# Later steps of x in 256-byte runs, a ring of three half units, one output tile, small ScalarE loads behind its copies

## The chip, the cores and the metric

One Trainium2 chip, one core. The metric is device time in microseconds (us) of one execution of the program, as the median of several runs. All data is float32; "f32r" tiles hold float32 values that TensorE reads in its one-pass float32 form.

## The reference, cut to what matters

x is [B=128, T=64, D=512]; `cond` is [128, 512] and serves twice: as the 128 taps of a depthwise causal convolution and as the initial state of a GRU.

```python
x = x + (depthwise_causal_conv(x, taps=cond[:, None, :]) + conv_b)   # 128 taps over 64 time steps
gi = x_t @ W_ih + b_ih ; gh = h @ W_hh + b_hh                         # for t in 0..63, one after the other
r = sigmoid(i_r + h_r); z = sigmoid(i_z + h_z); n = tanh(i_n + r * h_n)
h = (1 - z) * n + z * h
out[:, t] = x_t + h
```

Here x_t is the x after the convolution. The 64 GRU steps depend on each other through h; the convolution depends on nothing but the input.

## The kernel before, in words

**GRU steps.** Each of the 64 steps multiplies the state and the next step's x with two 512 x 1536 matrices. Every float32 product is done as three TensorE matmuls on a high and a low part (hi*hi, hi*lo, lo*hi; `block_product`, L775 to L781). A step is 24 groups of three matmuls of 512 columns, 72 in all, on L779, and four transposes of h (L741). ScalarE makes the high part of h and of the next x (L605, L571), the sigmoids and the tanh (L578, L591, L586), and puts the biases into the PSUM banks (L519). VectorE makes the low parts (L617), the gate arithmetic (L697 to L708), the residual sum `outT` (L723) and its transposition `outZ` (L730). SP stores outZ in four DMAs (`store_out`, L402) and loads the x of the step four ahead in four more (`load_early_xT` L328, `load_xT` L336). There are two `outZ` tiles used in turn; a transposition waits for the store of two steps earlier.

**Time steps 0 to 15 of the convolution (the early part)** are computed before the first step, 64 channel groups on TensorE (L768, 16 banks of 4 groups), from a Toeplitz tile that ScalarE and VectorE build out of the taps (L500, L641). The taps go through DRAM first: `tap_pad` is stored and `tap_blocks` loaded by ScalarE's DMA queue (L467 to L472), which then also issues four loads of `bias_d` (L476) and two of `bias_pair` (L481), before ScalarE's first copy (L485). The results are stored to `early` in DRAM in four quarters (L325) and come back transposed as xT(t) (L330).

**Time steps 16 to 63 (the bulk)** are computed between the matmuls of GRU steps t = 1 to 13. Channels go in pairs (two channels are stacked on the 128 partitions, 64 time steps each), two pairs to a PSUM bank: 128 banks m = 0 to 127, ten to a step, at the points p = 0 to 9, which come after 3, 5, 8, 10, 12, 15, 17, 20, 22 and 24 of the 24 groups (the transposes of h stand after the 20th). m = 10 (t - 1) + p. `bulk` (L786) issues four matmuls for a bank (L801). A **block** j is four pairs, that is banks 2j and 2j + 1. For each block

- SP loads the Toeplitz matrices from DRAM in two DMAs of 128 KB, runs of 256 bytes (`load_toep`, L352, L358), into a ring of four; the load for block m/2 + 3 is issued at bank m;
- ScalarE rounds x to its high part (L551) and VectorE subtracts to get the low part (L668), `split(j)`, into a ring of three; at bank m = 2j - 4, whose point in the step is even;
- each bank is emptied by ScalarE (L561, two halves into `tmp`, adding the bias) and VectorE (L679, into `stage`); TensorE may use bank m when bank m - 3 has been emptied.

x comes in **units**: 32 pairs, that is 2 x 32 channels, in 8 DMAs of 256 KB (`load_x_quarter`, L343, L347), so runs of 32 channels = 128 bytes, into two tiles `x_unit` used in turn. Units 0 and 1 are loaded before the loop; quarters of a later unit go out one at a time at every second bank, from the bank at which the unit two back has been split. `stage` holds eight banks, twice; `store_stage` (L364) writes it to `xres` in DRAM in two DMAs at banks m with m % 8 == 2, the stage of the eight banks before, and VectorE waits for the store of two stages back before it writes the first bank of a new one (L677).

**Order on SP.** SP's program is one list: at each point of step t the bulk loads and stores above (each behind its wait on `conv_done`, which counts finished banks), then `store_out(t)` behind the wait for outZ, then the x of step t + 4. Before the loop: xT(1), unit 0 of x (8 DMAs), four toeps (8), xT(2) and xT(3) (8), unit 1 of x (8).

**Order on ScalarE at the points** (VectorE's is the same with `second_half`): p0: split, first_half; r and its bias; first_half(p1); split(p2), first_half(p2); wait for the pre-activation, tanh, bias of i_n; first_half(p3); wait for the z product, z, two biases; split(p4), first_half(p4), first_half(p5); split(p6), first_half(p6); split(p8), first_half(p7); high part of h; first_half(p8).

Of the kernel before, what the change touches and what calls it, by code (L numbers as in the profile page):

```python
# [5 lines left out]
P = 128  # L6
# [3 lines left out]
ACT = mybir.ActivationFunctionType  # L10
# [9 lines left out]
def conv_residual_gru(  # L20
# [26 lines left out]
    KB = D // P  # L47
# [12 lines left out]
    UNIT = 32  # L60
    NUNIT = PAIRS // UNIT
    STAGE = 16
# [37 lines left out]
    x_unit = [place(f"x_unit{n}", B * UNIT) for n in range(2)]  # L100
# [10 lines left out]
    xT2, xT3 = place("xT2", D), place("xT3", D)  # L111
    gru_end = top[0]
    xT0, xT1 = place("xT0", D), place("xT1", D)
# [14 lines left out]
    top[0] = toep_at  # L128
# [4 lines left out]
    assert top[0] <= gru_end  # L133
# [18 lines left out]
    with ctx:  # L152
# [48 lines left out]
        x_unit_loaded = [sem(f"x_unit_loaded{n}") for n in range(2)]  # L201
# [29 lines left out]
        out_stored = [sem(f"out_stored{n}") for n in range(2)]  # L231
# [53 lines left out]
        def x_block(j):  # L285
            c0 = j % (UNIT // BLOCK) * BLOCK
            unit = j // (UNIT // BLOCK) % 2
            return x_unit[unit][:, :].rearrange("p (b g) -> p g b", g=UNIT)[:, c0:c0 + BLOCK, :]

        def part_block(j, low):  # L290
            return parts[j % HL_RING][:, :].rearrange("p (g l b) -> p g l b", l=2, b=B)[:, :, low, :]
# [4 lines left out]
        def _(sp):  # L296
# [81 lines left out]
            for b4 in range(4):  # L378
                load_x_quarter(0, b4)
# [4 lines left out]
            for b4 in range(4):  # L384
                load_x_quarter(1, b4)

            def bulk(t, point):
# [491 lines left out]
```

## Time and profile before

| what | us |
|---|---|
| median of 3 runs | 1238.42 (1237.55 to 1242.0) |
| the profiled execution: its time | 1239.42 |
| the profiled execution: its span | 1237.5 |
| TensorE matmul busy in the span | 1182.9 (96%) |
| TensorE weight load busy | 986.4 (80%) |
| VectorE / ScalarE busy | 539.3 / 500.2 |
| data moved | 97.98 MB in 288354 packets, 212752 of them under 512 bytes |

Time outside the span is 1.9 us. Engines in the rows below: PE is TensorE's matmuls, PEld its weight loads, DVE VectorE, ACT ScalarE, POOL GpSimd, SPq and ACTq the DMA issues of SyncE and ScalarE. L779 is line 779 of the kernel. A PSUM bank appears as "bank". Each window row gives the stretch, its length, then busy us (and instructions) of PE, PEld, DVE, ACT and POOL, the mean granted TensorE clock (1.00 is 2.4 GHz), the busy share of the 16 DMA engines and GB/s.

### The profile page before, as it was taken

The numbers are of one execution on the slowest core, as the hardware profiler recorded it, in microseconds if no ns is written. First come the engines' busy times: TensorE is split into PE (matmuls) and PEld (weight loads), VectorE is DVE, ScalarE is ACT, GpSimd is POOL, SyncE is SP. The second block draws the span as 40 slices with busy tenths as digits, with TensorE's granted clock in tenths as the row PEclk, the third lists the DMA queues.
The fourth block names the chain that finished last, engine by engine and source line by source line (L and its number), as shares of the span: only waits on it lengthen the run. The fifth ranks groups of instructions, "written<-read, shape, count | busy, mean of one in ns | idle before, by whom it ended". The sixth has DMA issues, their size and how long they took to land.

```text
span 1237.5 us, 15341 instructions
## 1 busy us (share of the span) xinstructions
PE 1182.9 (96%) x5518; PEld 986.4 (80%) x5518; DVE 539.3 (44%) x811; ACT 500.2 (40%) x934; POOL 17.2 (1%) x19
## 2 busy tenths in 40 slices
PE   1997999899989999999999999999999999999997
PEld 1976788787878888888888888888888888888886
DVE  2835766476655333333333333333333333333333
ACT  4436766576755333323333323333332333332332
POOL 0400000000000000000000000000000000000000
PEclk9999999899989999999999999999999999999999
DMA  9978888788853111111011111001111101111100
GB/s 244 293 176 161 167 173 175 170 183 174 173 149 77 54 32 35 34 34 32 24 29 34 34 34 34 25 25 34 34 34 34 28 24 34 34 34 34 32 17 21
DMA packets 288354, 97.98 MB, mean 79 GB/s; under 512 B 212752, under 2 KB 282384, under 8 KB 286272
## 3 DMA queue, kind: packets, MB, share of 16 engines
q1 hardware_dynamic: 283968, 96.29, 33.1%
q10 hardware_dynamic: 4352, 1.25, 0.4%
q8 instruction: 20, 0.33, 0.1%
q14 instruction: 14, 0.11, 0.0%
HBM read 63.34 MB, written 34.14 MB: 79 GB/s over the span
## 4 chain that ended last, share of the span: by engine, by line
PE 89%; ACT 3%; issue 2%; SPq 2%; DMA 2%; DVE 2%; ACTq 0%; DVEq 0%
PE bank L779 80%; PE bank L801 4%; PE bank L741 2%; PE bank L768 2%; SPq L347 1%; ACT tmp L561 1%; ACT x_parts L551 1%; SPq L358 1%; DMA early<-early_result 1%; ACT bank L519 0%; ACT toep_early L500 0%; DMA xres<-stage 0%; DVE stage L679 0%; DVE x_parts L668 0%; DMA tap_pad<-tap_rows 0%
## 5 line engine op out<-in xcount | busy, mean ns | idle before, releaser
L779 PE MATMUL bank<-w_ih_hi,xT_hi 128*128 128x512 f32 x768 | 308.2, 401 | 0.0
L779 PE MATMUL bank<-w_ih_hi,xT_lo 128*128 128x512 f32 x768 | 302.2, 394 | 0.0
L779 PE MATMUL bank<-w_ih_lo,xT_hi 128*128 128x512 f32 x768 | 302.2, 393 | 0.0
L779 PE MATMUL bank<-w_hh_hi,hT_hi 128*128 128x512 f32 x768 | 299.6, 390 | 0.0
L779 PE MATMUL bank<-w_hh_lo,hT_hi 128*128 128x512 f32 x768 | 299.5, 390 | 0.0
L779 PE MATMUL bank<-w_hh_hi,hT_lo 128*128 128x512 f32 x768 | 298.8, 389 | 0.0
L779 PEld LDWEIGHTS bank<-w_ih_hi,xT_lo 128*128 128x128 f32 x768 | 145.6, 190 | 31.8
L779 PEld LDWEIGHTS bank<-w_hh_hi,hT_lo 128*128 128x128 f32 x768 | 144.2, 188 | 30.4
L779 PEld LDWEIGHTS bank<-w_ih_hi,xT_hi 128*128 128x128 f32 x768 | 146.1, 190 | 27.2 <-ACT bank L519 0.4
L779 PEld LDWEIGHTS bank<-w_ih_lo,xT_hi 128*128 128x128 f32 x768 | 146.1, 190 | 26.8
L779 PEld LDWEIGHTS bank<-w_hh_hi,hT_hi 128*128 128x128 f32 x768 | 144.4, 188 | 28.1
L779 PEld LDWEIGHTS bank<-w_hh_lo,hT_hi 128*128 128x128 f32 x768 | 144.4, 188 | 27.6
L617 DVE TENSOR_TENSOR hT_lo<-bank,hT_hi 128x512 fp32r<-128x512 f32 x64 | 44.1, 688 | 219.7 <-ACT hT_hi L605 219.3
L697 DVE TENSOR_TENSOR q<-bank,r 128x512 f32<-128x512 f32 x64 | 44.2, 690 | 204.6 <-PE bank L779 203.4
L605 ACT ACTIVATE hT_hi<-bank 128x512 fp32r<-128x512 f32 x63 | 37.7, 599 | 206.1 <-PE bank L741 206.1
L586 ACT ACTIVATE n_gate<-q 128x512 f32<-128x512 f32 x64 | 40.5, 633 | 172.6 <-DVE q L699 172.6
L801 PEld LDWEIGHTS bank<-x_parts,toep_ring 128*128 128x128 f32 x512 | 79.4, 194 | 36.7 <-issue 20.1
L801 PE MATMUL bank<-x_parts,toep_ring 128*128 128x256 f32 x512 | 84.6, 289 | 22.0 <-issue 18.2
L561 ACT ACTIVATE tmp<-bank,bias_pair 128x128 f32<-128x128 f32 x256 | 78.3, 364 | 54.8 <-PE bank L801 54.5
L571 ACT ACTIVATE xT_hi<-xT 128x512 fp32r<-128x512 f32 x63 | 39.8, 632 | 123.6 <-PE bank L779 108.3
L668 DVE TENSOR_TENSOR x_parts<-x_unit,x_parts 128x512 fp32r<-128x512 f32 x64 | 70.2, 1097 | 44.7 <-ACT x_parts L551 44.6
L551 ACT ACTIVATE x_parts<-x_unit 128x512 fp32r<-128x512 f32 x64 | 73.8, 1155 | 24.0 <-PE bank L801 21.2
(59 smaller groups left out, 802.3 us busy)
## 6 DMA issues: line engine op xcount, KB each, us to landing
x_unit<-in_x_dram SPq DMA_DIRECT2D x64, 256.0 KB, 4.7
toep_ring<-kernel_parts SPq DMA_DIRECT2D x128, 128.0 KB, 3.3
out_dram<-outZ SPq DMA_DIRECT2D x256, 64.0 KB, 1.6
xres<-stage SPq DMA_DIRECT2D x32, 384.0 KB, 5.0
xT<-xres SPq DMA_DIRECT2D x192, 64.0 KB, 1.9
early<-early_result SPq DMA_DIRECT2D x4, 1024.0 KB, 13.8
xT<-early SPq DMA_DIRECT2D x60, 64.0 KB, 2.0
w_ih_raw<-in_L_cond_W_ih_dram SPq DMA_DIRECT2D x12, 256.0 KB, 7.8
```

Of the source, the lines that this page charges most:

```text
L551: nc.scalar.activation(part_block(j, 0), x_block(j), ACT.Copy).then_inc(x_hi_ready, 1)
L561: nc.scalar.activation(tmp[m % 2][:, pair * B:(pair + 1) * B], conv_bank[m % 3][:, pair * 2 * B:pair * 2 * B + B], ACT.Identity, bias=bias ...
L571: nc.scalar.activation(xT_hi[:, :], xT[(u + 1) % RING][:, :], ACT.Copy).then_inc(xT_hi_ready, 1)
L586: nc.scalar.activation(n_gate[:, :], q[:, :], ACT.Tanh).then_inc(n_ready, 1)
L605: nc.scalar.activation(hT_hi[:, :], ps_hT[:, :], ACT.Copy).then_inc(hT_hi_ready, 1)
L617: nc.vector.tensor_tensor(lo_out[:, :], full[:, :], hi_in[:, :].bitcast(F32), ALU.subtract).then_inc(lo_ready, 1)
L668: nc.vector.tensor_tensor(part_block(j, 1), x_block(j), part_block(j, 0).bitcast(F32), ALU.subtract).then_inc(x_lo_ready, 1)
L697: nc.vector.tensor_tensor(q[:, :], ps_hn[:, :], r[:, :], ALU.mult).then_inc(reset_h_ready, 1)
L741: mm = nc.tensor.transpose(psum[:, k * P:(k + 1) * P], source[:, k * P:(k + 1) * P], ident[:, :])
L768: mm = nc.tensor.matmul(conv_bank[n % 3][:, slot:slot + B], toep_early[:, g * P:(g + 1) * P], x_early[:, :].rearrange("p (b g) -> p g b", ...
L779: mm = nc.tensor.matmul(psum[:, :], a[:, rows], b[w][:, cols], start=False, stop=stop and n == 2, skip_group_check=True)
L801: mm = nc.tensor.matmul(conv_bank[m % 3][:, pair * 2 * B:(pair + 1) * 2 * B], toep[j % T_RING][:, at:at + P], parts[j % HL_RING][:, slot * ...
```

## The change

Four things.

1. **Units of 64 pairs.** UNIT goes from 32 to 64, so a run of x is 256 bytes and there are four units instead of eight. Instead of two unit tiles there is a ring of three tiles of half a unit, split over the batch (64 of the 128 rows each). A half is four DMAs of 512 KB, each with as many runs as one of before. Units use the tiles (0,1), (0,2), (1,2), (0,1). Before the loop go unit 0 (8 DMAs, where unit 0 of before had 8 smaller ones) and the second half of unit 1 (4 DMAs, in place of 8). Later halves go out four DMAs at once: the first half of unit 1 at bank 27, behind a wait for the low part of block 15; the first of unit 2 at bank 30; the second of unit 2 at bank 59, behind block 31; the first of unit 3 at bank 62; the second of unit 3 at bank 91, behind block 47. The first three blocks of units 1 to 3 are split 1, 2 and 3 banks ahead of their first bank instead of 4, so split(16), split(32), split(48) stand at banks 31, 63 and 95, points p1, p3 and p5. `x_block` and `part_block` get one more dimension for the two halves.
2. **STAGE goes from 16 to 8**: `stage` holds four banks, twice; its store is half as large and goes out at m % 4 == 2.
3. **Output tiles.** `outT` is the tile q, which the gates use too, and one `outZ` takes the place of two; VectorE waits for outZ of the step before ahead of q, and the transposition for the store of the step before.
4. **Before the loop.** ScalarE copies x_row (L485) ahead of its first DMA issues, and makes the copies of L489 to L493 ahead of the six small loads of `bias_d` and `bias_pair`. TensorE no longer waits for `y0_ready` before the early matmuls, only before the third bank, which is the PSUM bank that y0 is read from.

Cut to its core:

```diff
-    UNIT = 32
+    UNIT = 64
     NUNIT = PAIRS // UNIT
-    STAGE = 16
+    UNIT_BLOCKS = UNIT // BLOCK
+    HALF = B // 2 * UNIT
+    HALF_OF = ((0, 1), (0, 2), (1, 2), (0, 1))
+    HALF_USE = ((1, 1), (2, 1), (2, 2), (3, 3))
+    STAGE = 8
...
-    x_unit = [place(f"x_unit{n}", B * UNIT) for n in range(2)]
+    x_ring = place("x_ring", 3 * HALF)
...
-    outT = place("outT", D)
     r, z, n_gate, q = (place(n, D) for n in ("r", "z", "n_gate", "q"))
-    outZ = [place(f"outZ{n}", D) for n in range(2)]
+    outT = q
+    outZ = place("outZ", D)
...
         def split_block(t, point):
             m = bulk_bank(t, point)
-            if m is None or m % 2 or m // 2 + 2 >= NBLOCK:
+            if m is None:
                 return None
-            return m // 2 + 2
+            for j in (m // 2 + 2, (m + 3) // 2, (m + 1) // 2):
+                ahead = (1, 2, 3)[j % UNIT_BLOCKS] if j % UNIT_BLOCKS < 3 and j >= UNIT_BLOCKS else 4
+                if 2 * j - ahead == m and j < NBLOCK:
+                    return j
+            return None
...
-            def load_x_quarter(unit, b4):
-                for c in range(2):
-                    ch = unit * 2 * UNIT + c * UNIT
-                    bs = slice(b4 * B // 4, (b4 + 1) * B // 4)
-                    sp.dma_start(
-                        x_unit[unit % 2][c * T:(c + 1) * T, :].rearrange("s (b g) -> s b g", g=UNIT)[:, bs],
-                        x[bs, :, ch:ch + UNIT].rearrange("b s g -> s b g"),
-                    ).then_inc(x_unit_loaded[unit % 2], 16)
+            def load_x_half(unit, half):
+                n = HALF_OF[unit][half]
+                for part in range(2):
+                    b0 = half * B // 2 + part * B // 4
+                    for c in range(2):
+                        ch = unit * 2 * UNIT + c * UNIT
+                        cols = slice(n * HALF + part * HALF // 2, n * HALF + (part + 1) * HALF // 2)
+                        sp.dma_start(
+                            x_ring[c * T:(c + 1) * T, cols].rearrange("s (b g) -> s b g", g=UNIT),
+                            x[b0:b0 + B // 4, :, ch:ch + UNIT].rearrange("b s g -> s b g"),
+                        ).then_inc(x_half_loaded[n], 16)
...
-            for b4 in range(4):
-                load_x_quarter(0, b4)
+            for half in range(2):
+                load_x_half(0, half)
             for j in range(T_RING):
                 load_toep(j)
             load_early_xT(2)
             load_early_xT(3)
-            for b4 in range(4):
-                load_x_quarter(1, b4)
+            load_x_half(1, 1)
...
-                if m % 8 == 2 and m > 2:
-                    store_stage(m // 8 - 1)
-                unit, b4 = (m + 21) // 16, (m + 21) % 16 // 2
-                if m % 2 and 2 <= unit < NUNIT and b4 < 4:
-                    if b4 == 0:
-                        sp.wait_ge(x_lo_ready, (unit - 1) * UNIT // BLOCK)
-                    load_x_quarter(unit, b4)
+                if m % 4 == 2 and m > 2:
+                    store_stage(m // 4 - 1)
+                unit = (m + 5) // 32
+                if 1 <= unit < NUNIT:
+                    if (m + 5) % 32 == 0:
+                        sp.wait_ge(x_lo_ready, unit * UNIT_BLOCKS)
+                        load_x_half(unit, 0 if unit == 1 else 1)
+                    if (m + 5) % 32 == 3 and unit < NUNIT - 1:
+                        load_x_half(unit + 1, 0)
...
-                unit = j // (UNIT // BLOCK)
-                act.wait_ge(x_unit_loaded[unit % 2], 16 * 8 * (unit // 2 + 1))
+                if j % UNIT_BLOCKS == 0:
+                    for half in range(2):
+                        act.wait_ge(x_half_loaded[HALF_OF[j // UNIT_BLOCKS][half]],
+                                    16 * 4 * HALF_USE[j // UNIT_BLOCKS][half])
...
+                if isinstance(i, bass.RuntimeValue) or t > 0:
+                    dve.wait_ge(outZ_ready, t)
                 dve.wait_ge(gh_n_done, t + 1)
...
-                if isinstance(i, bass.RuntimeValue) or t >= 2:
-                    dve.wait_ge(out_stored[u % 2], 16 * QUADS * (2 * i + u // 2))
-                nc.vector.transpose(outZ[u % 2][:, :], outT[:, :]).then_inc(outZ_ready, 1)
+                if isinstance(i, bass.RuntimeValue) or t > 0:
+                    dve.wait_ge(out_stored, 16 * QUADS * t)
+                nc.vector.transpose(outZ[:, :], outT[:, :]).then_inc(outZ_ready, 1)
...
-            pe.wait_ge(y0_ready, KB)
             for g in range(G0):
                 n, slot = g * B // BANK, g * B % BANK
                 if slot == 0 and n >= 3:
                     pe.wait_ge(early_evicted, n - 2)
+                if slot == 0 and conv_bank[n % 3] is ps_x0 and n < 3:
+                    pe.wait_ge(y0_ready, KB)
```

## Rows read from the trace of the kernel before

**Rows 1.** The page's fourth section: the chain that ended last, by engine

```profile
PE 89%; ACT 3%; issue 2%; SPq 2%; DMA 2%; DVE 2%; ACTq 0%; DVEq 0%
```

**Rows 2.** Windows: steps 2 to 12 together, then steps 6, 7, 9 and 11

```profile
117.74:379.22 261.48, 247.24 (x1278) 210.20 (x1276) 165.25 (x265) 176.31 (x375) 0.00 (x0) 0.97 0.79 168
208.80:237.80 29.00, 24.45 (x117) 20.60 (x116) 14.98 (x25) 16.06 (x35) 0.00 (x0) 0.88 0.83 179
237.80:259.56 21.76, 21.76 (x117) 18.70 (x116) 15.03 (x25) 15.99 (x35) 0.00 (x0) 1.00 0.88 161
281.44:307.02 25.58, 23.53 (x117) 19.86 (x116) 15.00 (x25) 15.99 (x35) 0.00 (x0) 0.93 0.86 175
328.78:357.46 28.68, 24.34 (x118) 20.35 (x116) 15.02 (x25) 16.05 (x35) 0.00 (x0) 0.88 0.71 162
```

**Rows 3.** Timeline of PE in step 6; in brackets the idle time before

```profile
226.03 1.20 PE L801 MATMUL bank<-x_parts,toep_ring 128*128 128x256 f32 x4 [4.54 <-issue]
```

**Rows 4.** Timeline of SP's issues, step 6: start, us, what

```profile
216.65 3.77 SPq L404 DMA_DIRECT2D out_dram<-outZ  x4
...
222.39 1.26 SPq L358 DMA_DIRECT2D toep_ring<-kernel_parts  x2
223.70 1.08 SPq L369 DMA_DIRECT2D xres<-stage  x2
```

**Rows 5.** Waits of SP's queue: us in total, times, longest

```profile
SPq L358 <- PE bank L801: 25.1, 24, 2.8
```

**Rows 6.** Windows: DMA carries early results; x_unit only; toep_ring and xT

```profile
56.00:64.00 8.00, 8.00 (x37) 6.88 (x36) 7.40 (x10) 2.19 (x4) 5.18 (x3) 1.00 1.01 428
70.00:82.00 12.00, 12.00 (x56) 9.97 (x55) 4.90 (x8) 6.30 (x10) 0.00 (x0) 1.00 1.00 158
86.00:90.00 4.00, 3.57 (x20) 3.13 (x20) 1.31 (x2) 0.20 (x1) 0.00 (x0) 1.00 0.92 220
```

**Rows 7.** Tile x_unit: SP's issue durations (ns), and issue to landing

```profile
L347 SPq DMA_DIRECT2D x_unit<-in_x_dram x64: 617/1552/3213, 68.5 to 329.8; - x64
...
DMA to landing us min/median/max: 3.3/4.7/6.5
```

**Rows 8.** Timeline of ScalarE before the loop: ACTq issues, y0

```profile
9.98 4.13 ACTq L476 DMA_DIRECT2D bias_d<-in_L_cond_b_dram  x4
...
28.34 1.46 ACT L507 ACTIVATE xT<-bank,bias_d,k_full 128x128 f32<-128x128 f32 x4
```

**Rows 9.** Timeline of SP's issues from 68 us

```profile
68.46 12.15 SPq L347 DMA_DIRECT2D x_unit<-in_x_dram  x8
...
87.08 4.20 SPq L330 DMA_DIRECT2D xT<-early  x8
91.33 11.62 SPq L347 DMA_DIRECT2D x_unit<-in_x_dram  x8
...
107.98 3.98 SPq L358 DMA_DIRECT2D toep_ring<-kernel_parts  x6
```

**Rows 10.** Timeline of ScalarE: split(0) and split(1)

```profile
84.08 2.12 ACT L551 ACTIVATE x_parts<-x_unit 128x512 fp32r<-128x512 f32 x2 [2.86 <-DMA x_unit<-in_x_dram]
```

**Rows 11.** Timeline of PE: bulk banks 0 and 8

```profile
86.43 0.71 PE L801 MATMUL bank<-x_parts,toep_ring 128*128 128x256 f32 x4 [1.03 <-DVE x_parts L668]
...
111.73 0.81 PE L801 MATMUL bank<-x_parts,toep_ring 128*128 128x256 f32 x3 [4.87 <-issue]
```

**Rows 12.** Timeline of PE, step 7: bulk banks 62, 64 and 66

```profile
242.20 0.64 PE L801 MATMUL bank<-x_parts,toep_ring 128*128 128x256 f32 x4
...
245.92 0.64 PE L801 MATMUL bank<-x_parts,toep_ring 128*128 128x256 f32 x4
...
250.32 0.64 PE L801 MATMUL bank<-x_parts,toep_ring 128*128 128x256 f32 x4
```

**Rows 13.** Timeline of ScalarE, step 7: bias of i_n

```profile
245.86 0.58 ACT L519 ACTIVATE bank<-bias_in 128x512 f32<-128x512 f32 x1
```

**Rows 14.** Timeline of VectorE, step 7: the transposition of the output

```profile
257.69 0.71 DVE L730 STREAM_TRANSPOSE outZ<-outT 128x512 f32<-128x512 f32 x1
```

More of the change, by code:

```diff
@@ L199, in conv_residual_gru @@
         early_stored = [sem(f"early_stored{n}") for n in range(QUARTERS)]
-        x_unit_loaded = [sem(f"x_unit_loaded{n}") for n in range(2)]
+        x_half_loaded = [sem(f"x_half_loaded{n}") for n in range(3)]
         toep_loaded = [sem(f"toep_loaded{n}") for n in range(T_RING)]
@@ L230, in conv_residual_gru @@
         outZ_ready = sem("outZ_ready")
-        out_stored = [sem(f"out_stored{n}") for n in range(2)]
+        out_stored = sem("out_stored")
         ROUNDS = T // RING
@@ L285, in x_block @@
         def x_block(j):
-            c0 = j % (UNIT // BLOCK) * BLOCK
-            unit = j // (UNIT // BLOCK) % 2
-            return x_unit[unit][:, :].rearrange("p (b g) -> p g b", g=UNIT)[:, c0:c0 + BLOCK, :]
+            unit, g0 = j // UNIT_BLOCKS, j % UNIT_BLOCKS * BLOCK
+            first, second = HALF_OF[unit]
+            at = x_ring[:, first * HALF + g0:first * HALF + g0 + BLOCK]
+            return bass.AP(at.tensor, at.offset, [at.ap[0], [1, BLOCK], [(second - first) * HALF, 2], [UNIT, B // 2]])
         def part_block(j, low):
-            return parts[j % HL_RING][:, :].rearrange("p (g l b) -> p g l b", l=2, b=B)[:, :, low, :]
+            return parts[j % HL_RING][:, :].rearrange("p (g l h b) -> p g l h b", l=2, h=2, b=B // 2)[:, :, low]
         block = ctx.enter_context(nc.Block())
@@ L405, in store_out @@
                         out[:, bass.ds(t, 1), :].rearrange("(Q s) o (q e) -> q s Q (o e)", s=QUAD, e=P)[q4],
-                        outZ[u % 2][q4 * QUAD:(q4 + 1) * QUAD, :].rearrange("s (Q e) -> s Q e", e=P),
-                    ).then_inc(out_stored[u % 2], 16)
+                        outZ[q4 * QUAD:(q4 + 1) * QUAD, :].rearrange("s (Q e) -> s Q e", e=P),
+                    ).then_inc(out_stored, 16)
             def step(i, u):
@@ L429, in _ @@
             rounds(sp, step)
-            for n in range(2):
-                sp.wait_ge(out_stored[n], 16 * QUADS * T // 2)
+            sp.wait_ge(out_stored, 16 * QUADS * T)
         @block.gpsimd
@@ L464, in tap_columns @@
                 return tile[:, :].rearrange("p (k j) -> p k j", j=P)
+            act.wait_ge(x_row_loaded, 16)
+            nc.scalar.activation(x_row_by_k[:, :].rearrange("b (k q r) -> b q k r", k=KB, r=QUAD),
+                                 gate_in_order(x_row), ACT.Copy).then_inc(x_row_by_k_ready, 1)
             act.wait_ge(tap_zeros_set, 1)
@@ L474, in _ @@
                           ).then_inc(tap_blocks_loaded, 16)
+            act.wait_ge(hT_done, 1)
+            act.wait_ge(k_zeroed, 1)
+            nc.scalar.activation(tap_columns(k_full)[:, :, 0:T], tap_columns(ps_hT)[:, :, T:P],
+                                 ACT.Copy).then_inc(k_full_copied, 1)
+            nc.scalar.activation(hT_hi[:, :], ps_hT[:, :], ACT.Copy).then_inc(hT_hi_ready, 1)
+            act.wait_ge(k_full_ready, 1)
+            nc.scalar.activation(k_parts[:, :].rearrange("p (k l j) -> p k l j", l=2, j=P)[:, :, 0, 0:T],
+                                 tap_columns(k_full)[:, :, 0:T], ACT.Copy).then_inc(k_hi_ready, 1)
             for q4 in range(QUADS):
@@ L581, in step @@
                     put_bias(ps_r, bias_rz[:, R:R + D], bias_r_put)
+                split(split_block(t, 1))
                 first_half(bulk_bank(t, 1))
@@ L588, in step @@
                     put_bias(ps_in, bias_in[:, :], bias_in_put)
+                split(split_block(t, 3))
                 first_half(bulk_bank(t, 3))
@@ L597, in step @@
                 first_half(bulk_bank(t, 4))
+                split(split_block(t, 5))
                 first_half(bulk_bank(t, 5))
@@ L601, in step @@
                 split(split_block(t, 8))
+                split(split_block(t, 7))
                 first_half(bulk_bank(t, 7))
@@ L691, in step @@
                 second_half(bulk_bank(t, 0))
+                split(split_block(t, 1))
                 second_half(bulk_bank(t, 1))
@@ L699, in step @@
                 nc.vector.tensor_tensor(q[:, :], ps_in[:, :], q[:, :], ALU.add).then_inc(pre_n_ready, 1)
+                split(split_block(t, 3))
                 second_half(bulk_bank(t, 3))
@@ L710, in step @@
                 second_half(bulk_bank(t, 4))
+                split(split_block(t, 5))
                 second_half(bulk_bank(t, 5))
@@ L714, in step @@
                 split(split_block(t, 8))
+                split(split_block(t, 7))
                 second_half(bulk_bank(t, 7))
```

22 lines of the change are left out of this document (5 added, 17 removed).

## The prediction, made before the changed kernel ran

> **What bounds the kernel now.** I start with the chain that ended last: 89% of it is PE [rows 1]. So I look for the stretches in which PE isn't at its own pace. The stretches of the windows are GRU steps, each from its first bulk bank. A step with bulk work and no stall takes 21.76 us, PE busy throughout and the clock at 1.00 [rows 2]. Eleven of these would be 239.4 us; steps 2 to 12 took 261.48 us, so **22.1 us** are lost there, most of it in steps 6, 9 and 11 (7.2, 3.8 and 6.9) [rows 2]. The reader should see two losses in each: PE busy 24.45 of 29.00 us, so 4.55 idle, and a clock of 0.88, so about 2.7 more at half speed (1.2 instead of 2.4 GHz) [rows 2]. In every one PE stands ahead of a bulk bank, and the releaser is given as "issue" [rows 3], which is how a DMA that came last shows here.
>
> What was late? In step 6 PE stood before bank 56, idle to 226.03 [rows 3]. Its block 28 has its Toeplitz load in SP's program at bank 50, and that is the issue of 222.39, after store_out and xT(9) [rows 4]. SP is six banks behind. It isn't waiting: its issues follow one another without a gap [rows 4], and all its toep waits for banks come to 25.1 us in the whole kernel [rows 5]. SP is held by the DMA engines: an x issue takes 0.62 us at least, 1.55 in the median [rows 7], about the 1.66 us in which 262144 bytes move at the 158 GB/s of a stretch that carries only x with the DMA share at 1.00 [rows 6]. **The bulk is bound by SP's list, and SP by x in 128-byte packets.** From step 14 on nothing in the change can matter but the output tiles.
>
> **The change, part by part.**
>
> *Price of the new x DMA.* It has as many packets as the old one, of 256 bytes. Toep and xT traffic ran at 220 GB/s with a share of 0.92 [rows 6]; between that and the same at full share (239) a DMA of 524288 bytes takes 2.38 to 2.19 us. I take 2.3, so 32 x 2.3 = 74 us for x where 64 x 1.55 = 99 were: 25 us off SP's list. Bounds: 2.19 below; above, twice 1.66 = 3.3, if a packet's cost went by bytes alone, which the toep row speaks against. The Trainium skill ("DMA: Bandwidth & Descriptors", Why small descriptors are slow) counts 3 cycles per packet beside one per 32 bytes, 11 against 7 here; by that the DMA would take 1.66 x 11/7 = 2.6 us, an estimate, dearer than the toep row has it.
>
> *Between bursts.* From bank 0 to 27, 34 to 59 and 64 to 91 SP issues only toeps (1.26 us a pair), stores (1.08 a stage) and eight small DMAs a step: about 12 us in a 21.76 us step [rows 2, 4]. It keeps up; steps without a burst take 21.8.
>
> *Before the loop.* ScalarE's copies move ahead of small DMA issues, of which the four of bias_d alone take 4.13 us; y0 was finished at 29.80 [rows 8]. I expect the early matmuls 2 to 4 us sooner. This is hidden: the early stores drain at 428 GB/s with the DMA share at 1.01 [rows 6], and SP's first x issue at 68.46 [rows 9] waits for them. Price 0. Its cover is the DMA queue; PE will simply idle longer ahead of bulk bank 0.
>
> *Unit 0* is now 4 MB. The last of the eight landed at 84.08, when ScalarE's split began [rows 10], that is 68.46 + 8 x 1.66 + 2.3. Now: 68.46 + 8 x 2.3 + 2.3 = 89.2, 5.1 later. Split to matmul took 86.43 - 84.08 = 2.35 us [rows 10, 11], so bulk bank 0 starts at 91.5 instead of 86.43, after an idle time of some 7 us, thus with the clock at half for a while (1.7 us lost in a stretch of 3.4). SP is free of unit 0 about 3.8 later than at 80.6, but the next x burst is 4 x 2.3 us where eight DMAs took 11.62 [rows 9]; the toep of bank 8 is issued at about 106 instead of 107.98 [rows 9]. PE waited 4.87 us for it until 111.73, then ran at half clock for 3.4 us (1.7 lost) [rows 11]. Now it arrives at 91.5 + 17.4 (eight banks at a clean pace) + 1.7 + 1 (waits for ScalarE) = 111.6 and finds it landed. Effect up to there: 111.6 - (111.73 + 1.7) = **-1.8 us**, between -5 and +3.
>
> *Three bursts.* Only the three unit borders can stall now. A half lands 4 x 2.3 + 2 = 11.2 us after its first issue (2 is between 2.3 and the least landing, 3.3, less 1.66 [rows 7]). Offsets are from the step's first bank, 237.80 in step 7.
> - Border 1: block 15 is split at p6, 12.52 + 2.35 = 14.9 into step 3 [rows 12]; then x is issued, lands 26.1 = 4.3 into step 4; bank 32 starts at 6.7 instead of 4.40 [rows 12]: 2.3 us. The next burst, at bank 30, puts 9.2 us of x ahead of two toeps and two stage stores; with stages of four banks the store has only some 6 us, so VectorE is held at the first bank of stages 8 and 9, about 2.5 us for PE. Half clock 1.7. Sum 6.5.
> - Border 2: split(32) stands at p3, behind the tanh and the bias of i_n, which ends 8.64 in [rows 13]; the half (issued at about 18 into step 6) landed at 7.4. Bank 64 starts at 8.64 + 2.35 = 11.0 instead of 8.12 [rows 12]: 2.9 us. Half clock 0.8. Sum 3.7. No load can help this one.
> - Border 3: outZ ends 20.6 in [rows 14], 1.2 before step 10; then store_out 1.8, xT 2.1 (half of 4.20 [rows 9]), toep 1.26, stage 1.08: x goes out 5.2 into step 10, lands at 16.4, and bank 96 starts at 18.7 instead of 12.52 [rows 12]: 6.2 us. Half clock 2.5 (2.7 in step 6 after 4.5 us idle). Sum 8.7.
>
> Together **18.9 us in place of 22.1: -3.2**. Added splits at odd points fall in these steps alone.
>
> *Output tiles.* VectorE's wait for outZ ahead of q is for its own instruction of 8 us before: 0. The transposition waits for the store of one step earlier, issued 15 us before; behind it stand the last emptying of a bank and the next low part of x. SP's lag in a burst is at most 10 us: 0, at worst 1. If that is wrong, the 50 steps without bulk work would show it.
>
> Strided reads of x go from 128 to 256 bytes apart; the split takes 1.06 us on ScalarE [rows 10]. Between 0.6 and 1.3 us nothing changes but 0.2 us at each border.
>
> **Sum**, against the profiled execution's 1239.42 (span 1237.5 and 1.9 around it): -1.8 - 3.2 = -5.0, 1234.4. The median shown is 1.0 lower, so **1233.5 us**.
>
> **Rivals.**
> - *Bursts cost little* (1224). ScalarE and VectorE have slack and the half lands at 2.19 us a DMA: border 1 costs 1, border 2 its 2.9, border 3 5.0, clock losses 3 in all, 12 instead of 18.9, and the start gives 4 instead of 1.8. For: the toep row at full share. Against: SP's order at border 3 is fixed, and in step 9 even 2.05 us of idle time (25.58 less 23.53) came with a clock of 0.93, some 1.7 us [rows 2].
> - *Slow packets* (1238.5): x at 2.6 us a DMA, between the 2.38 and 3.3 of the bounds. Unit 0 lands 8 x 0.3 = 2.4 later, borders 1 and 3 come 1.2 later each, and one more stretch of half clock weighs at most 1.7 us: 5 us with what ScalarE adds, and the gain is gone. The Trainium skill's section named above gives just this price. For: x comes with a stride of 2 KB, the toep rows don't. Against: the rate of 220 to 239.
> - *The halved stage holds VectorE* (1247.5, slower). Place: the wait for the stage's store, behind the double bursts at banks 27/30 and 59/62. A store has 6 us from its issue point to its use where it had 15. If SP comes out of a burst over 10 us late (x issues at the 3.2 us maximum [rows 7] instead of 2.3 make eight of them 7 us longer), VectorE stands before the first bank of a stage, and the gates and the low part of h stand behind it: 5 us more in each of two double bursts, and 2 of clock with each: 14 us, and 1233.5 + 14 is 1247.5. It decides from a lag of SP of about 10 us on. For: ScalarE, VectorE and SP are in order. Against: TensorE may run three banks ahead.
> - *No gain because SP wasn't the bound*: would show as 1238; rows 4 and 5 leave it little.
>
> **How the numbers follow.** A change under 0.5% (6.2 us) can't be told from none. Forecast, own range 1228 to 1239: 0.45, of it just under half beyond -0.5%. Bursts cheap: 0.2. Slow packets or no gain: 0.17. Stage: 0.18. Faster 0.2 + 0.2 = 0.40; same 0.25 + 0.16 = 0.41; slower 0.19. The range of 1221 to 1245 takes in the forecast, the cheap bursts and the slow packets, and leaves out most of the stage case.
>
> **What would show it.** Right: step windows of 21.8 for 2, 3, 5, 8, 9, 11, 12 and of 25 to 31 for 4, 7 and 10; SP idle, waiting for conv_done, between bursts; bulk bank 0 near 91.5 and no stall at bank 8; x rows at 215 to 240 GB/s; steps of the loop unchanged at 16.8. Wrong: clean steps over 22, VectorE's stage row released by "DMA xres" for more than 9 us in all, or bank 96 starting within 3 us of its clean place.

## The result and the profile after

The changed kernel takes **1256.07 us** (median of 4 runs, 1255.49 to 1256.37) beside 1240.21 for the kernel before on the same chip: ratio **1.0128**, 95% interval 1.0102 to 1.0153. It is 16 us slower. The prediction said 1233.5 and gave "slower" 0.19; the rival of the halved stage had said 1247.5.

The windows by step of the changed kernel, for [rows 2]: steps 2 to 12 together, then steps 2, 3, 4, 8 and 10, and last a stretch in which eight x DMAs run alone. The columns are those of [rows 2].

```profile
116.32:395.90 279.58, 249.46 (x1277) 208.04 (x1276) 165.36 (x269) 173.74 (x375) 0.00 (x0) 0.97 0.62 150
116.32:142.44 26.12, 22.79 (x118) 18.37 (x116) 17.18 (x29) 15.58 (x35) 0.00 (x0) 1.00 0.44 121
142.44:164.20 21.76, 21.76 (x118) 18.72 (x116) 14.21 (x24) 14.17 (x33) 0.00 (x0) 1.00 0.70 162
164.20:197.36 33.16, 26.20 (x118) 20.63 (x116) 16.50 (x27) 17.70 (x36) 0.00 (x0) 0.90 0.88 195
...
269.29:296.52 27.23, 23.14 (x117) 18.38 (x117) 17.17 (x29) 15.29 (x34) 0.00 (x0) 1.00 0.52 139
318.26:352.20 33.94, 24.19 (x118) 20.05 (x116) 14.36 (x25) 16.18 (x35) 0.00 (x0) 0.85 0.65 150
...
70.00:84.00 14.00, 12.27 (x45) 9.92 (x45) 5.46 (x8) 4.90 (x9) 0.00 (x0) 0.76 1.16 220
```

Steps 2 to 12 take 279.58 us where they took 261.48; a clean step is still 21.76, so 40.2 us are lost instead of 22.1. Step 2 begins 1.42 us earlier than before. The steps grew by 279.58 - 261.48 = 18.1 us; 18.1 - 1.4 = 16.7 us, and the span grew by 1254.2 - 1237.5 = 16.7: everything lies between step 2 and step 12. From the end of the last bulk bank to the end of the program both kernels take 842.6 us.

The step windows already contradict the prediction in one point: step 2 and step 8 have no border, and lose 4.4 and 5.5 us at a clock of 1.00, with a DMA share of only 0.44 and 0.52. The DMA engines were busy for about half of these steps, so bandwidth is not what is short there. The waits by engine, queue of SP and VectorE (us in total, times, longest), tell more:

```profile
DVE stage L698 <- DMA xres<-stage: 42.7, 10, 7.6
```

```profile
SPq L418 <- DVE outZ L754: 663.6, 61, 15.0
SPq L371 <- PE bank L826: 49.5, 23, 5.8
```

SP now waits 49.5 us for banks before Toeplitz loads, where it waited 25.1 [rows 5]: the change did free SP's list, as meant. (A part of the 49.5 is TensorE's own standing; in the run with the early store below, as fast as the kernel before, it is 35.0.) But VectorE stands 42.7 us for its own stage store, 9.0 before. The timeline of SP in steps 1 and 2 shows how a store comes to be late:

```profile
95.15 7.08 SPq L360 DMA_DIRECT2D x_ring<-in_x_dram  x4
102.27 3.72 SPq L418 DMA_DIRECT2D out_dram<-outZ  x4
106.03 1.90 SPq L340 DMA_DIRECT2D xT<-early  x4
107.97 3.98 SPq L371 DMA_DIRECT2D toep_ring<-kernel_parts  x6
111.99 1.08 SPq L382 DMA_DIRECT2D xres<-stage  x2
113.12 1.41 SPq L371 DMA_DIRECT2D toep_ring<-kernel_parts  x2
119.20 1.79 SPq L418 DMA_DIRECT2D out_dram<-outZ  x4
121.04 1.88 SPq L340 DMA_DIRECT2D xT<-early  x4
122.96 1.26 SPq L371 DMA_DIRECT2D toep_ring<-kernel_parts  x2
124.26 1.08 SPq L382 DMA_DIRECT2D xres<-stage  x2
```

and the timeline of VectorE beside it (the first two lines empty banks 3 and 7, the last of stages 0 and 1):

```profile
104.15 0.42 DVE L698 TENSOR_TENSOR stage<-bank,tmp 128x256 f32<-128x256 f32 x1 [1.73 <-ACT tmp L576]
...
111.40 0.42 DVE L698 TENSOR_TENSOR stage<-bank,tmp 128x256 f32<-128x256 f32 x1
...
117.41 0.43 DVE L698 TENSOR_TENSOR stage<-bank,tmp 128x256 f32<-128x256 f32 x1 [5.00 <-DMA xres<-stage]
...
118.46 0.71 DVE L754 STREAM_TRANSPOSE outZ<-q 128x512 f32<-128x512 f32 x1
...
128.02 0.42 DVE L698 TENSOR_TENSOR stage<-bank,tmp 128x256 f32<-128x256 f32 x1 [5.28 <-DMA xres<-stage]
```

Read them together. SP comes out of the last x burst before the loop (95.15 to 102.23) with a list that it works off without a gap, so the store of stage 0, full at 104.57, goes out at 111.99, 7.4 us late. VectorE stands 5.00 us for it, so it transposes step 1's output late (118.46). SP's next entry is the output store, which waits for that transposition (119.20). Behind it stand xT, a Toeplitz load and only then the next stage store (124.26), although its stage had been full since 111.82, 12.4 us before. VectorE needs that buffer and stands again, 5.28 us. So VectorE's wait delays SP, and SP's delay makes VectorE wait: with stages of eight banks there was mostly time for this between store and reuse, with four there is not. TensorE runs up to three banks ahead and then stands too; in the timeline of PE, for bank 15 and for a product with the next step's x, whose bias ScalarE puts late:

```profile
128.50 0.74 PE L826 MATMUL bank<-x_parts,toep_ring 128*128 128x256 f32 x4 [1.36 <-DVE stage L698]
130.97 0.50 PE L804 MATMUL bank<-w_ih_hi,xT_hi 128*128 128x512 f32 x1 [1.05 <-ACT bank L532]
```

Step 8 has the same pattern, behind the x burst of bank 62. In SP's timeline:

```profile
255.49 7.68 SPq L360 DMA_DIRECT2D x_ring<-in_x_dram  x4
...
267.61 1.08 SPq L382 DMA_DIRECT2D xres<-stage  x2
...
273.36 1.78 SPq L418 DMA_DIRECT2D out_dram<-outZ  x4
...
278.42 1.08 SPq L382 DMA_DIRECT2D xres<-stage  x2
```

VectorE stands 7.60 us for the store of 267.61 and 5.21 for that of 278.42. Steps 2 and 8 have no burst of their own, but they begin before SP has caught up from one: the Toeplitz load at their first bank goes out 8.5 and 12.2 us after the bank before has ended. In steps 3, 5, 6, 9, 11 and 12 this lag is 4.5 to 6.7 us, and with the store in the same place they lose at most 0.4 us each. The borders cost more than forecast as well. Timelines of SP, ScalarE and PE at the third border (bank 96), to be set beside the clean pace of [rows 12]:

```profile
324.25 8.32 SPq L360 DMA_DIRECT2D x_ring<-in_x_dram  x4
```

```profile
337.46 1.06 ACT L566 ACTIVATE x_parts<-x_ring 128x512 fp32r<-128x512 f32 x1 [4.65 <-DMA x_ring<-in_x_dram]
```

```profile
339.74 1.19 PE L826 MATMUL bank<-x_parts,toep_ring 128*128 128x256 f32 x4 [8.64 <-DVE x_parts L687]
```

The half is split 13.2 us after its first issue, and PE has then been idle for 8.64 us.

### The profile page after: what moved, and what is told of

The parts are those of the page before. It is cut to its first block, busy times and chain, and to the rows that moved or that the text cites. A ratio compares the mean times of both kernels' runs of the same rounds, so it can differ in the third digit from the quotient of the medians.

```text
span 1254.2 us, 15299 instructions
## 1 busy us (share of the span) xinstructions
PE 1187.4 (95%) x5518; PEld 986.5 (79%) x5518; DVE 535.6 (43%) x811; ACT 497.7 (40%) x934; POOL 16.7 (1%) x19
## 4 chain that ended last, share of the span: by engine, by line
PE 82%; SPq 5%; DMA 4%; ACT 3%; DVE 3%; issue 2%; ACTq 0%; DVEq 0%
PE bank L804 75%; PE bank L826 3%; PE bank L793 2%; SPq L360 2%; PE bank L765 2%; SPq L371 2%; DMA xres<-stage 2%; ACT x_parts L566 1%; DMA x_ring<-in_x_dram 1%; DVE x_parts L687 1%; DMA early<-early_result 1%; SPq L340 1%; ACT tmp L576 0%; ACT bank L532 0%; ACT toep_early L513 0%
## 5 line engine op out<-in xcount | busy, mean ns | idle before, releaser
L698 DVE TENSOR_TENSOR stage<-bank,tmp 128x256 f32<-128x256 f32 x128 | 52.4, 418 | 89.9 <-ACT tmp L576 47.1
L586 ACT ACTIVATE xT_hi<-xT 128x512 fp32r<-128x512 f32 x63 | 39.8, 632 | 124.6 <-PE bank L804 109.5
L687 DVE TENSOR_TENSOR x_parts<-x_ring,x_parts 128x512 fp32r<-128x512 f32 x64 | 68.8, 1077 | 44.9 <-ACT x_parts L566 43.8
```

Source lines behind the costliest of these rows:

```text
L586: nc.scalar.activation(xT_hi[:, :], xT[(u + 1) % RING][:, :], ACT.Copy).then_inc(xT_hi_ready, 1)
L687: nc.vector.tensor_tensor(part_block(j, 1), x_block(j), part_block(j, 0).bitcast(F32), ALU.subtract).then_inc(x_lo_ready, 1)
L698: nc.vector.tensor_tensor(stage[s % 2][:, at:at + 2 * B].rearrange("p (g b) -> p g b", b=B), conv_bank[m % 3][:, :].rearrange("p (g l b) - ...
```

## The experiments

Theory A after the first comparison: the stage store's place in SP's list behind the output store, together with the halved stage, costs some 16 us; what is left of the loss is the landing of the half at each border. All ratios are to the kernel before on the same chip, with their 95% intervals. "Lost" is what steps take over 21.76 us each. The kernel before took 1243.86 us on the chip of the first four runs, 1240.89 on that of the early store, half the bytes, the second burst spread with GpSimd's stores and GpSimd's stores on the kernel before, and 1239.46 on that of the other four. So ranges in us that start from a run on another chip are up to 4.4 us off, and the ratios decide. Waits and lost us are those of the one profiled execution of a run, which can lie some us off its median.

### The three parts alone

**Halved stage on the kernel before** (space held so that no other tile moves):

```diff
-    STAGE = 16
+    STAGE = 8
-                if m % 8 == 2 and m > 2:
-                    store_stage(m // 8 - 1)
+                if m % 4 == 2 and m > 2:
+                    store_stage(m // 4 - 1)
```

> The kernel before with the stages alone halved (four banks, store at m % 4 == 2), x and everything else as before. Theory A, the halved stage: VectorE waits for a stage's store behind SP's late list, as in the changed kernel, where that wait is 42.7 us in 10 places against 9.0 in 2. SP is late through the whole bulk here, so it costs at least as much as there: 1250 to 1265 us. Rival B, the x bursts: the stages are harmless while x goes out one quarter at a time, 1238 to 1243 us.

Measured: 1264.76 us, ratio **1.0169** (1.0152 to 1.0186); steps 2 to 12 lost 49.0 us. The wait of VectorE:

```profile
DVE stage L680 <- DMA xres<-stage: 85.2, 17, 10.0
```

One constant, which the prediction costed at nothing between bursts, is alone worth more than the whole loss (21 us against 16). On the kernel before, where SP is late through the whole bulk, it is even dearer than in the changed kernel. (The profiled execution took 1269.01 us, the longest of the four.)

**Output tiles alone** (outT shares q's tile, one outZ; the wait for outZ moves ahead of q):

```diff
-    outT = place("outT", D)
-    outZ = [place(f"outZ{n}", D) for n in range(2)]
+    outT = q
+    outZ = place("outZ", D)
```

> The kernel before with the output tiles alone changed (outT in q, one outZ). Both theories: nothing, within 3 us of before, and the steps without bulk at 16.80 us. Rival C: the transposition waits for the store of the step before where SP is late in the bulk, which would show as VectorE idle before the transposition and 3 to 8 us more.

Measured: 1244.85 us, ratio 1.0009 (0.9998 to 1.0020). Nothing, as predicted.

**The part before the loop alone** (ScalarE's copies ahead of its small DMA issues; the wait for y0 moved to the first bank that overwrites it):

```diff
-            pe.wait_ge(y0_ready, KB)
             for g in range(G0):
...
+                if slot == 0 and conv_bank[n % 3] is ps_x0 and n < 3:
+                    pe.wait_ge(y0_ready, KB)
```

> The kernel before with the part before the loop alone changed (ScalarE's copies ahead of its small loads, TensorE's wait for y0 moved). The early matmuls start some 5 us sooner or more (23.5 against 29.95 in the changed kernel); SP's first x issue moves from 68.46 to about 67. Theory: most of it is hidden behind the DMA engines, gain 1 to 2 us. Rival: the gain reaches bank 8, 4 us or more.

Measured: 1242.59 us, ratio 0.9989 (0.9977 to 1.0001). The early matmuls started at 24.48 instead of 29.95 us, bulk bank 0 at 87.26 instead of 86.43: the first are 5.5 us sooner (2 to 4 were forecast), SP's first x issue stands at 68.72 instead of 68.46, and so the gain is hidden behind the early stores, as predicted. At most some 3 us of the whole (0.23%, the interval's end) can come of it.

### The store's place

**Stage stores issued by GpSimd**, all else as changed:

```diff
-                if m % 4 == 2 and m > 2:
-                    store_stage(m // 4 - 1)
...
+            for n in range(NBANK * 2 // STAGE):
+                store_stage(pool, n)
```

> The changed kernel with the stage stores issued by GpSimd, which has nothing else to do there, instead of standing in SP's list; sizes and waits the same. Theory A: the store goes out as soon as the stage is full, VectorE's waits for it fall from 42.7 us to under 10, steps 2 and 8 come out clean (21.8), the borders lose about half: 1232 to 1242 us. Rival B, the x bursts fill the DMA engines and the stores wait there just as long: 1250 us or more, with VectorE still released by the stores.

Measured: 1244.86 us, ratio 1.0015 (0.9998 to 1.0032). No wait of VectorE for a store is left, steps 2 and 8 take 21.8 us, and 27.2 us are lost, 7.8, 7.3 and 12.1 of them in steps 4, 7 and 10. The mechanism is A's; its range of 1232 to 1242 us was missed by 3 us, of which the chip explains most (the kernel before took 1243.86 on it), and the borders did not lose half.

**The same store two banks earlier in SP's list:**

```diff
-                if m % 4 == 2 and m > 2:
+                if m % 4 == 0 and m > 2:
                     store_stage(m // 4 - 1)
```

> The changed kernel with each stage store two banks earlier in SyncE's list, right behind that bank's Toeplitz load. Theory A (the halved stage is held by where its store stands in SyncE's list: behind the next output store, which itself waits for VectorE): the store is issued about two banks, some 4.4 us, sooner, so that VectorE's waits for stage stores fall from 42.7 us in 10 to under 15 us, steps 2 to 12 lose some 27 to 32 us instead of 40.2, and the time is 1243 to 1249 us. Rival B (a stage of 8 blocks is too small wherever its store stands: transfer and turn-round alone exceed the four banks it has): VectorE's waits stay above 30 us and the time stays at 1253 to 1257 us.

Measured: 1240.31 us, ratio **0.9996** (0.9986 to 1.0005), 3 us under the range of A and far from B. The wait of VectorE, and the windows of steps 2 to 12, 4 and 10:

```profile
DVE stage L698 <- DMA xres<-stage: 12.8, 4, 4.9
```

```profile
117.46:379.24 261.78, 245.67 (x1277) 209.15 (x1276) 164.75 (x267) 174.67 (x375) 0.00 (x0) 0.97 0.68 161
...
160.99:189.69 28.70, 24.06 (x118) 19.85 (x116) 15.29 (x26) 17.88 (x36) 0.00 (x0) 0.94 0.97 211
303.87:335.72 31.85, 23.73 (x118) 19.87 (x117) 14.35 (x25) 16.16 (x35) 0.00 (x0) 0.89 0.66 147
```

261.78 - 239.4 = 22.4 us are lost in place of 40.2, all of them in steps 4, 7 and 10, which is fewer than A's 27 to 32. A stage of eight is not too small in itself; its store stood in the wrong place. VectorE's 12.8 us of waits that are left fall in steps 1, 4 and 7, behind x bursts. In SP's timeline the store that the changed kernel issued at 124.26 now goes ahead of the output store:

```profile
115.72 1.08 SPq L382 DMA_DIRECT2D xres<-stage  x2
117.74 1.81 SPq L418 DMA_DIRECT2D out_dram<-outZ  x4
```

**GpSimd's stores on the kernel before** (stages of 16, x in quarters, with the part before the loop):

> The kernel before (quarters of 128-byte runs, stages of 16, two output tiles) with its stage stores issued by GpSimd and the ScalarE operations before the loop ordered as in the changed kernel. Theory A (the store's place behind SyncE's list costs VectorE even the 9.0 us in 2 waits of the kernel before, of which some reach TensorE): the waits go, steps 2 to 12 lose 15 to 19 us instead of 22.1, and the time is 0.2 to 0.6% under the kernel before, ratio 0.994 to 0.998. Rival B (with a stage of 16 the store is hidden, and SyncE's x quarters are the whole loss): ratio 0.998 to 1.001.

Measured: 1240.65 us, ratio 0.9993 (0.9975 to 1.0012), within B. With stages of 16 the store's place is worth nothing that can be measured.

### Is it the bursts or the single output tile?

**The second burst spread**, store in the change's place. The four DMAs of the next unit's first half are issued one each second bank, 35 to 41 and 67 to 73:

```diff
-                    if (m + 5) % 32 == 3 and unit < NUNIT - 1:
-                        load_x_half(unit + 1, 0)
+                    if 7 <= (m + 5) % 32 < 15 and m % 2 and unit < NUNIT - 1:
+                        sp.wait_ge(conv_done, m)
+                        load_x_half(unit + 1, 0, only=((m + 5) % 32 - 8) // 2)
```

> The changed kernel with the second half of a unit's pair issued one DMA each second bank, eight to fourteen banks after the border's, instead of as a burst of four; stage stores stay where the change has them in SyncE's list. Theory A (the stage waits come from the store's place behind the output store of the same step, whatever x does): steps 2 and 8, which no burst touches, still lose about 4.4 and 5.5 us, VectorE waits over 30 us for stage stores in all, and the time is 1249 to 1255 us. Rival B, as the prediction placed the stage's rival (the halved stage is late where two bursts of x hold SyncE): with the second burst spread, VectorE's waits fall under 20 us and the time is 1241 to 1247 us.

Measured: 1247.57 us, ratio 1.0062 (1.0042 to 1.0082); VectorE waited 28.1 us in 8 for stores. Neither theory's numbers hold. Step 2 lost 2.9 us; the two kernels issue the same up to bank 30, so this differs between executions (4.4 in the changed kernel, 3.6 in the run with two output tiles below). Step 8 fell from 5.5 to 1.4 and step 4 from 11.4 to 6.3. So the burst does push the ring of waits into stalling, and the late place makes it able to: removing either gives time back, and only removing the place gives all of it.

**The second burst spread, GpSimd's stores:**

> Stage stores issued by GpSimd, and the second half of a unit's pair is no longer issued three banks after the border's as one burst of four DMAs but one DMA each second bank, eight to fourteen banks into it. Theory A (two bursts of four 512 KB DMAs together cost mainly the first, waited-for one; the second costs banks 38 and 70 about 1 us each): those two waits go, border costs stay, time 1242 to 1244 us beside 1244.9. Rival B (the second burst delays Toeplitz loads, stores and output so that the borders' steps lose 3 us or more each by it): steps 4 and 7 fall from 7.8 and 7.3 us to under 4.5 and the time to 1236 to 1239 us.

Measured: 1240.36 us, ratio 0.9993 (0.9979 to 1.0006); 22.8 us lost in steps 4, 7 and 10 (5.4, 5.8, 11.6). The waits of banks 38 and 70 are gone. The time is 1.6 us below A's range, but that range started from 1244.9 us on another chip; as ratios to the kernel before it is 0.9985 to 1.0001, and A holds. The two bursted steps went a part of B's way: 2.4 and 1.5 us less, not 3. Against GpSimd's stores alone (1.0015) this is 0.2%, and the two intervals overlap.

**Two output tiles in the changed kernel:**

```diff
-    outZ = place("outZ", D)
+    outZ = [place(f"outZ{n}", D) for n in range(2)]
```

> The changed kernel with a second output tile (its addition still writes into q), which takes the change's output part back. Theory A (the single output tile costs nothing, here too: what SyncE stands behind is the transpose that has not yet run, not the store before it): 1254 to 1258 us, VectorE's stage waits 38 to 47 us. Rival B (the single output tile closes the ring of waits between VectorE, SyncE's output store and its stage store): stage waits under 25 us and 1244 to 1251 us.

Measured: 1253.13 us, ratio 1.0101 (1.0079 to 1.0124); VectorE waited 39.8 us for stage stores, as A had it; the time is 0.9 us under A's range. The interval overlaps that of the changed kernel: the output tile is not what closes the ring. Not shown is whether it adds a microsecond or two to it.

### The borders

**Half of the waited-for half**, with GpSimd's stores. Of the half a border waits for, each DMA brings 16 of its 32 batches; the rest keeps old values, so that part of the convolution is left out:

```diff
-                            x[b0:b0 + B // 4, :, ch:ch + UNIT].rearrange("b s g -> s b g"),
+                            x[b0:b0 + B // 4 // keep, :, ch:ch + UNIT].rearrange("b s g -> s b g"),
...
-                        load_x_half(unit, 0 if unit == 1 else 1)
+                        load_x_half(unit, 0 if unit == 1 else 1, keep=2)
```

> Stage stores issued by GpSimd, and each of the four DMAs of the x half that a border waits for brings 16 batches instead of 32; the other batches of that half are left out and old values are convolved in their place. Theory A (what is left of the loss, 27.2 us in steps 4, 7 and 10, is the landing of a half that is asked for only when the unit before it is split to the end): the half lands about 4.8 us sooner (4 x 1.2 us less), banks 32 and 64 start without their waits of 3.9 and 4.1 us, bank 96 waits under 4 us, steps 4, 7 and 10 lose 8 to 15 us together and the time falls from 1245 to 1227 to 1234 us. Rival B (the splits' place in ScalarE's and VectorE's lists, or the reduced clock, sets the borders, and transfer time does not): steps 4, 7 and 10 keep over 20 us and the time stays above 1238 us.

Measured: 1231.44 us, ratio 0.9922 (0.9906 to 0.9939). Steps 4, 7 and 10 lost 1.8, 4.4 and 5.9, together 12.1 instead of 27.2, as A had it. The split of bank 96's block ran 8.0 us after the first issue instead of 13.2, and PE waited for that bank as follows:

```profile
313.00 0.71 PE L825 MATMUL bank<-x_parts,toep_ring 128*128 128x256 f32 x4 [2.72 <-DVE x_parts L686]
```

So the landing sets borders 1 and 3. On border 2 A was half right: bank 64's wait fell from 4.14 to 2.55 us and no further, here and in both kernels with two passes below. There ScalarE's tanh and bias of i_n stand ahead of the split, which the prediction had ("No load can help this one", 2.9).

**Two passes by channels**, which loads everything and is a candidate. On top of the early store: at a border the waited-for half comes first for the unit's first 32 channels of each group (four DMAs of 128-byte runs), then the other 32, one DMA each second bank; then the next half, likewise spread. ScalarE waits for the rest before a unit's ninth block (not shown). The core of the edit:

```diff
+                        for which in range(4):
+                            load_x_some(unit, 0 if unit == 1 else 1, which, 0, None)
+                    at = (m + 5) % 32
+                    if at in (2, 4, 6, 8):
+                        sp.wait_ge(conv_done, m)
+                        load_x_some(unit, 0 if unit == 1 else 1, at // 2 - 1, 1, x_rest_loaded)
+                    if at in (10, 12, 14, 16) and unit < NUNIT - 1:
+                        sp.wait_ge(conv_done, m)
+                        load_x_some(unit + 1, 0, at // 2 - 5, None, None)
```

> A candidate: the stage store two banks earlier in SyncE's list; the half that a border waits for comes in two passes, four DMAs of 128-byte runs with the unit's first 32 channels of each group at once, the other four one each second bank; the pair's second half one DMA each second bank after them. Theory A (the border is set by the landing of the waited-for bytes): 4 x 1.66 us instead of 4 x 2.38 us, 2.9 us sooner at each border; steps 4, 7 and 10, which lost 22.3 us with the early store alone, lose 10 to 15 us and the time is 1230 to 1236 us, ratio 0.992 to 0.997. Rival B (SyncE, with eight DMAs of 2048 runs a border, is late with Toeplitz loads again as in the kernel before, up to one bank period for each): new waits of TensorE for Toeplitz blocks, 1238 to 1246 us.

Measured: **1227.34 us**, ratio **0.9912** (0.9884 to 0.9941). It beats both kernels: 0.9% under the one before, and by the two ratios (0.9912 / 1.0128 = 0.979) 2.1% under the changed one. The time is under A's range; the ratio's interval overlaps A's. Timelines of SP, ScalarE and PE at the third border, and the windows of steps 2 to 12 and 10:

```profile
301.52 5.40 SPq L361 DMA_DIRECT2D x_ring<-in_x_dram  x4
```

```profile
310.04 1.06 ACT L587 ACTIVATE x_parts<-x_ring 128x512 fp32r<-128x512 f32 x1 [2.03 <-DMA x_ring<-in_x_dram]
```

```profile
312.31 0.71 PE L847 MATMUL bank<-x_parts,toep_ring 128*128 128x256 f32 x4 [2.98 <-DVE x_parts L708]
```

```profile
115.11:366.55 251.44, 242.41 (x1278) 206.74 (x1276) 164.96 (x267) 174.36 (x375) 0.00 (x0) 0.99 0.72 167
...
296.65:323.02 26.37, 22.28 (x117) 18.69 (x116) 14.37 (x24) 16.14 (x35) 0.00 (x0) 1.00 0.81 162
```

The split follows the first issue by 8.5 us; steps 2 to 12 lose 251.44 - 239.4 = 12.1 us. Of B there is a trace: SP's list is full again after a border, and bank 46 waits 1.61 us, put down to "issue", for a Toeplitz load that stands behind step 4's output store. Two things differ from the run with the early store, the passes and the spread second burst; the next run tells them apart.

**The same with GpSimd's stores:**

> The same two passes and spread, with the stage stores issued by GpSimd instead of two banks earlier by SyncE. Theory A (the same gain of 2.9 us a border from 27.2 us in steps 4, 7 and 10): 1233 to 1239 us. Rival B (late Toeplitz loads): 1240 to 1246 us. Where SyncE is the limit, this kernel is faster than the other candidate by having fewer entries in SyncE's list; where it is not, the two agree within 2 us.

Measured: 1232.19 us, ratio 0.9928 (0.9905 to 0.9951). Over its base (1.0015) that is 0.9%, about 11 us, somewhat more than the 8.7 of A; the spread second burst is part of it. Against the run with the second burst spread and GpSimd's stores (0.9993, 0.9979 to 1.0006), which lacks only the two passes and has its spread DMAs two banks earlier, it is 0.65%, 8 us, with intervals that don't touch: that is what the passes are worth. Its interval overlaps that of the candidate above, so no order between the two is shown; in its trace (of the slowest of the four executions) bank 46 waited 3.46 us and bank 96 5.21, so that fewer entries in SP's list brought nothing visible.

## Why the prediction was wrong

- **What bounds the kernel** was right: SP's list, and the change relieved it (waits for banks 49.5 us instead of 25.1, and 35.0 in the run with the early store). But with the early store the whole is only as fast as before: what SP's list no longer cost, the borders did.
- **Price of the x DMA**: 2.3 predicted. The eight DMAs of unit 0 alone ran at 220 GB/s, 524288 bytes in 2.38 us, the upper end of 2.19 to 2.38 and the toep row's own rate. The Trainium skill ("DMA: Bandwidth & Descriptors", Why small descriptors are slow) would have made it 2.6, an estimate; the trace is 0.2 under that.
- **Before the loop, 0**: right by its own run, within its interval. **Output tiles, 0**: right by its own run.
- **Unit 0**: bulk bank 0 at 91.5 predicted, 90.87 measured; idle before it about 7, measured 5.58; step 2 at -1.8, measured -1.42. Right, with some luck: SP's first x issue came at 66.91 instead of 68.46, and from there to the first split it took 21.7 us, not 20.7. Bank 8 didn't find its way free, as forecast, but waited 0.94 us for VectorE.
- **Between bursts, "it keeps up"**: this is the step that failed. It added up SP's work ("about 12 us in a 21.76 us step"; its own rows give 5 x 1.26 + 2.5 x 1.08 + 3.9 = 12.9) and never asked whom SP waits for. In steps 3, 5, 9 and 11 it did keep up (21.8 us). In steps 2 and 8, which it wanted clean too, it did not: 26.12 and 27.23 us. SP came out of a burst late and had the time to catch up, but spent it waiting for an output store that VectorE had not yet transposed, with the stage store behind it. By the run with the early store, the late place costs 40.2 - 22.4 = 17.8 us in steps 2 to 12: 4.4 in step 2, 4.5 in step 4, 6.4 in steps 7 and 8, 2.1 in step 10 and 0.5 elsewhere. The sum had 2.5 for it, inside border 1's 6.5.
- **The rival of the halved stage** named the right wait and nearly the right condition, that SP comes out of a burst some 10 us late (8.5 and 12.2 us at the start of steps 2 and 8; the stage stores of 124.26, 267.61 and 278.42 went out 12 to 15 us after their stages were full). It looked only at the two double bursts, which with the steps behind them cost some 11 of its 14 us; the burst before the loop (step 2) and border 3 it left out. The prediction had even written "A store has 6 us from its issue point to its use", and its sign for being wrong, more than 9 us of waits for stores, came out at 42.7.
- **Three borders, 18.9**: with the early store they cost 22.3 (6.9, 5.3, 10.1; predicted 6.5, 3.7, 8.7), so this term is 3.4 too small. Banks 32, 64 and 96 waited 2.90, 2.77 and 7.01 us there (predicted 2.3, 2.9, 6.2). At border 2 the wait was right and the clock wrong: 3.4 us at half speed, 1.7 lost where 0.8 stood, and 0.58 more at bank 70. A half was split 12.4 to 13.2 us after its first issue in the changed kernel, 11.8 to 12.5 with the early store, not 11.2: four DMAs take 9.5 at 2.38, the forecast's 2 us of landing make 11.5, and 0.3 to 1.7 us more passed. That Toeplitz, xT and stage transfers issued just before share the DMA engines would fit, but wasn't isolated. The run with half the bytes shows that the landing is the cause at borders 1 and 3. "No load can help this one" was nearly right for border 2: its split still waited 0.91 us for the landing in the changed kernel, and none with half the bytes.
- The forecast and the terms found add up to 1234.4 + 17.8 + 3.4 + 0.4 (start) = 1256.0, beside 1256.36 for the profiled execution. That is bookkeeping, since 17.8 and 3.4 come from the same traces; what confirms the first by itself is the ratio, 1.0128 against 0.9996, 16.4 us.

## What to carry to other kernels

When a buffer in a ring is halved, follow its release through the issuing engine's list entry by entry, and ask of each entry ahead of it whom it waits for; free time on that queue says little. Start where the queue is latest, behind a burst, and look at the step after the burst too. A store that frees a buffer goes ahead of entries that wait for the engine which needs that buffer. Larger runs make each DMA cheaper by the byte, but where one is waited for, only the bytes needed first should be in front: 128-byte runs for the first half of the channels beat 256-byte runs for all of them, by 0.65% (0.9928 against 0.9993).

## What the runs showed of the hardware

- A stage store took 5.4 us from its first issue to VectorE's release (111.99 to 117.41), with a DMA share of 0.72 in that stretch; the median from issue to landing of these stores is 3.1 us, the longest 4.7. Of the 6 us that the halved ring has from issue point to reuse, 1.3 to 2.9 us are left for a late issue.
- The x read of 256-byte runs reached a DMA share of 1.16 at 220 GB/s; the 128-byte runs of before reached 1.00 at 158 [rows 6]. Doubling the run raised the rate by a factor of 1.39.
- A stage store pair issued by GpSimd held it 1.03 us, about as long as SP (1.08), and nothing else waits there. In that run the stores went out as soon as their stages were full, and the median to landing was the same 3.1 us.
- Idle time of about the same length had different effects on the granted clock. In the fastest kernel 2.98 us of it before bank 96 left the step at 1.00 (the last window above), and 2.55 us before bank 64 were followed by 3.41 us at half speed (window below); before, 2.05 us in step 9 came with 0.93 [rows 2]. A price per stall, as the prediction used, holds only roughly.

```profile
239.09:242.50 3.41, 3.41 (x11) 2.81 (x10) 3.34 (x5) 2.29 (x4) 0.00 (x0) 0.50 0.93 170
```
